# A Mamba scan phase with decays and half of h in PSUM, B times u on GpSimd, and a sum over states by accumulating transposes

## The reference

```python
def _mamba_block(x, ...):                    # 4 blocks: 0 then 1 forward, 2 then 3 backward
    xz = layer_norm(x) @ in_w                # 256 -> 2 x 512
    xs, z = split(xz)
    xc = silu(causal depthwise conv of 4 taps (xs) + conv_b)
    delta = softplus(xc @ xd_w @ dtp_w + dtp_b)          # 512 channels
    Bm, Cm = xc @ xB_w, xc @ xC_w                        # 16 states
    dA = exp(delta[..., None] * A)
    dBx = (delta * xc)[..., None] * Bm[:, :, None, :]
    h[t] = dA[t] * h[t-1] + dBx[t];  y[t] = sum over n of h[t, :, n] * C[t, n]
    return (y + D * xc) * silu(z) @ out_w + x
```

## Time and profile before

| | value |
|---|---|
| median of 3 runs | 11924.65 us (11923.49 to 11926.36) |
| the profiled execution | 11928.52 us, its span 11926.8 us |
| first scan to last scan of the Mamba phase | 116.9 to 10202.7 us |
| busy share over the span | DVE 89%, PE 84%, PEld 66%, ACT 51%, POOL 1% |
| mean granted TensorE clock | 0.919 of full speed |

### The profile page before, as it was taken

The page is one execution under the profiler, slowest core; times in us unless marked ns, Lnnn a source line. Parts: engine busy times, 40 slices in busy tenths (PEclk is TensorE's granted clock), DMA queues, the critical chain, the costliest instruction groups (busy, mean ns, idle before and its releaser), DMA issues. The chain is left out here.

```text
span 11926.8 us, 119277 instructions
## 1 busy us (share of the span) xinstructions
PE 10008.6 (84%) x40728; PEld 7855.0 (66%) x40728; DVE 10590.5 (89%) x8817; ACT 6109.2 (51%) x9969; POOL 94.9 (1%) x167
## 2 busy tenths in 40 slices
PE   7888888888888888888888888888888887799998
PEld 5666666666666666666666666666666666577776
DVE  6999999999999999999999999999999999333332
ACT  4555555555555555555555555555555554244443
POOL 0000000000000000000000000000000000000000
PEclk8999999999999898999999989999999998899999
DMA  2211122222211122212221222222221221000000
GB/s 79 76 63 59 68 77 71 70 72 70 76 64 63 64 76 71 77 67 75 71 69 50 76 71 75 69 70 75 71 69 57 67 71 65 22 11 11 11 11 9
DMA packets 357680, 728.02 MB, mean 61 GB/s; under 512 B 143670, under 2 KB 188890, under 8 KB 357082
## 3 DMA queue, kind: packets, MB, share of 16 engines
q1 hardware_dynamic: 343128, 683.98, 17.1%
q0 software_dynamic: 10240, 33.56, 0.8%
q10 hardware_dynamic: 3714, 2.89, 0.1%
HBM read 699.27 MB, written 21.05 MB: 60 GB/s over the span
## 5 line engine op out<-in xcount | busy, mean ns | idle before, releaser
L896 PE MATMUL y_ps<-hb,ident 128*128 128x257 f32 x16384 | 4489.7, 422 | 1478.3 <-DVE hb L692 1471.4
L896 PEld LDWEIGHTS y_ps<-hb,ident 128*128 128x128 f32 x16384 | 3286.5, 207 | 2497.1 <-DVE hb L692 1987.9
L683 DVE TENSOR_TENSOR_SCAN hb<-decay,hb 128x1028 f32<-128x1028 f32 x2048 | 4697.0, 2293 | 22.9 <-issue 22.2
L506 ACT ACTIVATE decay<-delta,neg_a 128x512 f32<-128x512 f32 x4096 | 2681.8, 712 | 2531.5 <-DVE hb L683 1804.7
L692 DVE TENSOR_TENSOR hb<-hb,c_all 128x1028 f32<-128x1028 f32 x2048 | 2505.2, 1223 | 0.0
L673 DVE TENSOR_TENSOR hb<-b_all,u_buf 128x1028 f32<-128x1028 f32 x2048 | 2471.7, 1207 | 5.8
L787 PE MATMUL w_ps<-xn,in_w 128*128 128x257 f32 x4096 | 1040.3, 402 | 146.5 <-ACT xn L407 116.7
L787 PEld LDWEIGHTS w_ps<-xn,in_w 128*128 128x128 f32 x4096 | 819.4, 202 | 306.0 <-issue 131.3
L787 PE MATMUL w_ps<-xs_pad,diag_store 128*128 128x257 f32 x4096 | 954.8, 379 | 0.2
L787 PEld LDWEIGHTS w_ps<-xs_pad,diag_store 128*128 128x128 f32 x4096 | 774.1, 189 | 114.2 <-ACT diag_store L427 1.0
L787 PE MATMUL w_ps<-sz,out_w 128*128 128x257 f32 x2048 | 517.7, 397 | 0.8 <-DVE sz L700 0.8
(11 more groups left out here) (237 smaller groups left out, 9233.5 us busy)
## 6 DMA issues: line engine op xcount, KB each, us to landing
b_all<-bc_dram SPq DMA_DIRECT2D x512, 514.0 KB, 3.6
c_all<-bc_dram SPq DMA_DIRECT2D x512, 514.0 KB, 4.9
in_w<-in_L_attn_in_w SPq DMA_DIRECT2D x64, 1024.0 KB, 4.9
x_in<-in_x POOLq DMA_DIRECT2D x128, 256.0 KB, 2.8
out_w<-in_L_attn_out_w SPq DMA_DIRECT2D x64, 512.0 KB, 3.7
h_mid<-h_cur SPq DMA_DIRECT2D x32, 257.0 KB, 3.2
h_F<-h_mid SPq DMA_DIRECT2D x16, 514.0 KB, 3.7
out<-o_sb SPq DMA_DIRECT2D x64, 86.0 KB
```

The costliest lines, as they stand in the source:

```text
L506: last = func(decay[:, u % NDA, i, :, 1:S], delta[:, c, :, 1:S], ACT.Exp, scale=neg_a[:, k, c, NU * n + i:NU * n + i + 1])
L683: dve.tensor_tensor_scan(h, decay[:, u % NDA, :, :, :].rearrange("p n b s -> p (n b s)"), h, 0.0, ALU.mult, ALU.add).then_inc(scan_done, 1)
L896: last = pe.matmul(y_ps[c % 2][:, b, 0:S], ident[:, :], hb[:, u % NHB, i, b, :], start=False, stop=(n == PAIRS - 1 and i == NU - 1))
```

## The change

- `decay` and the h of even states (`h_ps`) move to PSUM, as single states without token 0: `decay` has two buffers (NDP = 2), `h_ps` one. ACT writes one state's decays per instruction, two states ahead, between two halves of each unit's other work (`after_even`, `after_odd`).
- The scan runs per state and image: 256 columns, with token 0's B u as the initial value (an SBUF column). Even states' h goes to `h_ps`, odd ones' to `ch` in SBUF (NPR = 8 buffers). `c_times_h` is one instruction of 512 columns per state, from `h_ps` or in place, into `ch`.
- B times u goes to POOL, one instruction of 514 columns per state (`bu`, NBU = 4 buffers). So do the third part of `step_size`, `delta_x`, the convolution's diagonal matrices, `skip_weights`, and token 0's output (`first_tokens`, with `first_gains` on DVE).
- PE adds a state by four accumulating transposes (`is_transpose`) of 128 x 128 blocks of `ch` into one PSUM bank `y_ps`; tokens are on its partitions. At the end of a chunk ACT copies it to `y_t` (`token_rows`), PE turns it back into a `w_ps` buffer (`channel_rows`, keys y0 to y3), and DVE's `output` reads that.
- The loads of x move from POOL's queue to SP's.

The core of the diff:

```diff
+STATES = CI * NST
+L = S - 1
+NBU, NPR, NDP = 4, 8, 2
+POOL_C = ()
+        for name, before in [("y2", "dt0"), ("y1", "cv1" if jj in (2, 4) else "xs2")] + [("y0", "cen0" if jj == 4 else "var")]:
+    def y_at(jj):
+        return (12 if jj == 4 else 9), 18, (26 if jj in (2, 4) else 25)
+        y_ps = ctx.enter_context(nc.psum_tensor("y_ps", [P, 4, P], F32))
+        h_ps = ctx.enter_context(nc.psum_tensor("h_ps", [P, NB * L], F32))
+        decay = ctx.enter_context(nc.psum_tensor("decay", [P, NDP, NB * L], F32))
...
 # SP, period
                     load_weights(jj + 1)
+                    if jj == 2 and not is_final(g):
+                        load_x(g, 4)
                     bring_bc(g, jj + 1)
...
 # POOL
+            def b_times_u(g, jj, s):
+                if positive(job_count(g, jj, STATES, s + 1 - NBU)):
+                    pool.wait_ge(scan_done, job_count(g, jj, STATES, s + 1 - NBU))
+                pool.tensor_tensor(bu[:, s % NBU, :, :]..., b_all[:, n // NU, n % NU, :, :]...,
+                                   u_buf[:, c % 2, :, :]..., ALU.mult).then_inc(b_done, 1)
+                for s in range(STATES):
+                    b_times_u(g, jj, s)
+                    if s in (7, 9):
+                        step_size(g, jj, (s - 3) // 2)
+                    if s % NST == 11 and s < 3 * NST:
+                        delta_x(g, jj, s // NST + 1)
+                    if s in (21, 25):
+                        conv_weights(g, jj + 1, (s - 21) // 4)
+                    if s == 61:
+                        step_size(g, jj + 1, 0)
+                        delta_x(g, jj + 1, 0)
...
 # ACT
+            def token_rows(g, jj, c):
+                act.wait_ge(y_added, job_count(g, jj, STATES, NST * (c + 1)))
+                func(y_t[:, :, :], y_ps[:, :, :], ACT.Identity).then_inc(y_t_ready, 1)
+            def decays(g, jj, s):
+                if positive(job_count(g, jj, STATES, s + 1 - NDP)):
+                    act.wait_ge(scan_done, job_count(g, jj, STATES, s + 1 - NDP))
+                func(decay[:, s % NDP, :]..., delta[:, c, :, 1:S], ACT.Exp,
+                     scale=neg_a[:, k, c, n:n + 1]).then_inc(decays_ready, 1)
             def period(g, jj, first, last):
                 for u in range(UNITS):
+                        decays(g, jj, NU * u + NDP)
+                    after_even(g, jj, u, first, last)
+                        decays(g, jj, NU * u + NDP + 1)
+                    after_odd(g, jj, u, first, last)
...
 # DVE
+            def scan(g, jj, s, b):
+                inside = s % NU == 0
+                h = h_ps[:, :] if inside else ch[:, s % NPR, :]
+                last = dve.tensor_tensor_scan(h[:, cols], decay[:, s % NDP, cols], bu[:, s % NBU, b, 1:],
+                                              bu[:, s % NBU, b, 0:1], ALU.mult, ALU.add)
+            def c_times_h(g, jj, s):
+                product = ch[:, s % NPR, :]
+                h = h_ps[:, :] if s % NU == 0 else product
+                dve.tensor_tensor(product..., h..., c_all[:, n // NU, n % NU, :, 1:], ALU.mult).then_inc(c_done, 1)
             def period(g, jj, first, last):
+                    scan(g, jj, s, 0)
+                    scan(g, jj, s, 1)
                     if size:
                         step_size(*size, 0)
+                    scan(g, jj, s + 1, 0)
+                        scan(g, jj, s + 1, 1)
+                        c_times_h(g, jj, s)
+                        c_times_h(g, jj, s + 1)
+                    if u in y_at(jj):
+                        output(g, jj, y_at(jj).index(u))
...
 # PE
+            def add_state(g, jj, s):
+                if n == 0:
+                        pe.wait_ge(y_t_ready, job_count(g, jj, CI, c))
+                    for b, half, k in blocks:
+                        pe.matmul(y_ps[:, k, :], xc[:, jj % 2, c, b, 1 + half * P:1 + (half + 1) * P], skip_diag[:, :],
+                                  start=(k == 0), stop=False, skip_group_check=True)
+                for b, half, k in blocks:
+                    last = pe.matmul(y_ps[:, k, :], ch[:, s % NPR, k * P:(k + 1) * P], ident[:, :], is_transpose=True,
+                                     start=False, stop=(n == NST - 1 and k == 3), skip_group_check=True)
+            def channel_rows(g, jj, c):
+                pe.wait_ge(y_t_ready, job_count(g, jj, CI, c + 1))
+                    pe.wait_ge(read_of(name, g, jj), nth(name, g, jj) - 1)
             def period(g, jj, first, last):
+                        add_state(g, jj, NU * u - 2)
+                        add_state(g, jj, NU * u - 1)
+                    if u in y_at(jj):
+                        channel_rows(g, jj, y_at(jj).index(u))
```

More of the change, by code:

```diff
@@ L49, in one_job @@
     def one_job(jj, more):
-        keys = [("tmean", 4)] if jj == 3 and more else []
+        keys = [("y3", jj - 1)]
+        keys += [("tmean", 4)] if jj == 3 and more else []
         keys += [("o0", jj - 1), ("o1", jj - 1)]
@@ L549, in prepare_back, with first_input_at, after_even @@
                 projections(g, jj)
+            def first_input_at(jj):
+                return {2: 15, 4: 16}.get(jj, 13)
+            def after_even(g, jj, u, first, last):
+                if u == 0:
+                    softplus_start(g, jj, 3)
+                if u == 1:
+                    softplus_log(g, jj, 2)
+                if u % PAIRS == 0 and not (first and u == 0):
+                    token_rows(g, jj - (u == 0), (u // PAIRS - 1) % CI)
+                if u in (4 + (jj == 3), 5 + (jj == 3)) and not first:
+                    stream_out(g, jj - 1, u - 4 - (jj == 3))
+                if jj == 3 and not last and u == 6:
+                    inverse_deviation("tok", g, 4)
+                if u in (gates_at(jj) + 2, gates_at(jj) + 4):
+                    c = u - gates_at(jj) - 2
+                    gate(g, jj, c)
+                    gate(g, jj, c + 1)
+                    act.preload_act_table_set(LOG_EXP)
+                if last:
+                    return
+                if u == norm_at(jj) + 1:
+                    centred(g, jj + 1, 0)
+                if u == norm_at(jj) + 2:
+                    inverse_deviation("job", g, jj + 1)
+                if u in (first_input_at(jj), conv_at(jj) + 5):
+                    conv_input(g, jj + 1, 0 if u == first_input_at(jj) else 2)
+                if u in (conv_at(jj) + 3, conv_at(jj) + 8):
+                    c = (u - conv_at(jj) - 3) // 5 * 2
+                    conv_output(g, jj + 1, c)
+                    conv_output(g, jj + 1, c + 1)
+                    act.preload_act_table_set(LOG_EXP)
+                if u == conv_at(jj) + 10:
+                    projections(g, jj + 1)
+                if u in (26, 27):
+                    softplus_start(g, jj + 1, u - 26)
+                if u == 28:
+                    softplus_log(g, jj + 1, 0)
+                if u == 31:
+                    softplus_start(g, jj + 1, 2)
@@ new lines, in after_odd @@
+            def after_odd(g, jj, u, first, last):
+                if u == 0:
+                    softplus_powers(g, jj, 3)
+                if u == 1:
+                    softplus_log(g, jj, 3)
+                if jj == 3 and not last and u == 4:
+                    square_tokens(g, 4)
+                if jj == 0 and u == 6 or jj == 4 and u == 8:
+                    start_backward(g, jj + 1)
+                if jj == 4 and u == 11:
+                    copy_h(g, 4)
+                if last:
+                    return
+                if u == norm_at(jj) + 1:
+                    centred(g, jj + 1, 1)
+                if u == (15 if jj == 4 else 12):
+                    gain_and_bias(g, jj + 1)
+                if jj == 2 and not is_final(g) and u in (13, 15):
+                    tokens(g, 4, (u - 13) // 2)
+                if u in (first_input_at(jj), conv_at(jj) + 5):
+                    conv_input(g, jj + 1, 1 if u == first_input_at(jj) else 3)
+                if u in (26, 27):
+                    softplus_powers(g, jj + 1, u - 26)
+                if u == 28:
+                    softplus_log(g, jj + 1, 1)
+                if u == 31:
+                    softplus_powers(g, jj + 1, 2)
@@ L907, in lead_in @@
+                last.then_inc(full_of("first", 0, 0), 1)
                 pe.wait_ge(setup_act, 7)
```

420 lines of the change are left out of this document (226 added, 194 removed).

## The result

The changed kernel takes 12334.5 us (12324.3 to 12338.4) against 11924.1: a ratio of 1.0343 with a 95% interval of 1.0325 to 1.0361. It is 3.4% slower, as forecast in direction; the size was forecast at half, 12130. The profiled execution took 12324.3, its span 12322.5.

What follows compares the result with a forecast made beforehand. VectorE was taken to bound the Mamba phase at 157.7 us per job; 133.4 + 12.5 + 5.0 + 6.0 + 4.0 = 160.9 gave 12130 us, own range 11700 to 12500, over all 10950 to 12750.

Steps and rivals of the forecast that it cites:

- DVE's own work: VectorE's instructions in a Mamba job without waits on other engines: 133.4 us per job against 157.7, a gain of 24.3.
- POOL's hold of the odd C h: The odd state's C h, both inputs in SBUF, delayed by POOL's product: 0.39 us per unit, 12.5 per job.
- waits for decays, with PE's clock: DVE waiting on ACT's longer blocks with two decay buffers, 5.0 us per job, plus 4.0 for PE's slower clock.
- waits for POOL's B u: POOL's queue in the Mamba phase: no bound, 6 us ahead with four buffers, costed at nothing.
- waits before outputs: Chunk 0's output(0) waits for channel_rows: 7.8 us in three of four jobs, 0.4 in the fourth, mean 6.0.
- a share of the overlap: The odd C h loses 0.47 of its 0.63 us overlap with POOL's product: 0.29 us per unit.
- The second reading: DVE's odd C h is held until 0.14 us before POOL's product ends: 0.48 us per unit.
- rival 2: Odd C h held the whole 0.63 us by POOL, 7.7 us per job more: 12620 us, chance 0.18.
- clock term: PE, idle more, runs conv units at half clock: 8 us per job, taken at half, 4.0 (ends 0 and 8).
- Utilisation: Expected in the profile: PE busy near 60% with a mean clock under 0.85, POOL near 60%.
- 1: Rival: smaller waits, POOL's overlap at its share or nil, PE at full clock; 11670 to 10590 us, chance 0.33.
- 3: Rival: a PSUM operand doesn't free DVE, so scans meet POOL's products; 13380, at worst 15220 us; chance 0.05.

Runs made afterwards that it cites:

- taking one away alone: Changed kernel with either output(0) of VectorE two units later (12300.1 us), or y1 taken after cv1 for blocks 2 and 4 (12269.0 us).
- taking the hold away: Changed kernel with GpSimd's B times u cut to 16 columns of 514: 11561.5 us, ratio 0.9694 to the kernel before.
- the ring: Changed kernel with decays, h and product in three PSUM banks, scan in place, C h behind the next state's first scan: 11610.0 us, ratio 0.9738.
- three moves after the ring: The three-bank kernel plus output(0) two units later, y1 behind cv1, outputs' waits on themselves one scan later; the fastest version: 11249.1 us, ratio 0.9433.
- the C h in the new order: Changed kernel with every C h issued behind a scan (C h of s-1, then of s, between scans): 12269.4 us, ratio 1.0293.

## Why the prediction was right in sign and short in size

The forecast's job of 160.9 us came to 163.9. Per job:

| term | forecast | measured | from |
|---|---|---|---|
| DVE's own work | 133.4 | 132.4 | what is left of 163.9 |
| POOL's hold of the odd C h | 12.5 | 16.5 | (1197 - 680) ns x 32 |
| POOL's hold of L821 | 0 | 1.1 | (1212 - 681) ns x 128 / 64 |
| waits for decays, with PE's clock | 9.0 | 8.1 | 516.2 / 64 |
| waits for POOL's B u | 0 | 0.5 | 33.9 / 64 |
| waits before outputs | 6.0 | 5.3 | 338.1 / 64 |
| sum | 160.9 | 163.9 | |

(680 ns is what an odd C h takes beside constants only. The outputs' waits on themselves, 67.2 / 64 = 1.05, are in the first line, in the forecast as in the measurement.)

- *The step that was mis-sized is the hold.* The earlier trace rows allowed two readings, a share of the overlap (0.29 per unit) and a hold until 0.14 us before POOL's end (given as 0.48, rightly 0.49); I took the middle, 0.39, which no mechanism gives. In the unit shown the product ends at 5022.73, 0.87 after the odd C h starts, and this takes 1.42 where 0.68 would do: 0.74, which is 0.13 before POOL's end. At the share of 0.47 it would be 0.41. The second reading is right, here and in the 1762 cases counted above. The remaining length is more than the forecast's 0.63 because this product takes 1.29 and not the 1.09 of the earlier trace rows. In two of four chunks it is the short one, and a clean hold is 0.54.

  The mean hold, 0.52, is lower than both since POOL's other work shifts its products: 271 odd C h take under 0.70, others meet only the end of a product. So the second reading's 0.49 would have given a time near 12335, and that would have been partly luck, longer holds and missed ones making up for each other.

  The Trainium skill (SBUF — State Buffer, Summary: rules for kernel authors) says that the second of the two fully blocks until the first has finished: the runs agree but for the last 0.13 us, in both directions (POOL's 1.63 beside a C h that began first). They also agree with the statement of the Trainium skill (SBUF — State Buffer, Who interferes with whom) that an instruction of GpSimd that only writes doesn't contend. That was rival 2; its mechanism is the one that holds, its time of 12620 was too high for the mean hold.
- *POOL's hold of `step_size`*, 1.1 per job, was in no term: L821 on `cen` and `sq` has two SBUF inputs as well, and I had counted only the C h.
- *DVE's own work* was right: scans of 723 and 738 ns, 0.65 apart (forecast 0.66), and 0.58 between the two products (0.60). A unit without the hold takes 3.77 (forecast 3.84). That is in line with a pointer initial value at the 0.05 of the earlier trace rows, though no run left it out, and a PSUM result costs 0.015 us at most.
- *The output of chunk 0* was right in place and near in size: 335 of the 338 us stand there, in one wait per job, 5.6 to 7.2 on average in three of four jobs (forecast 7.8) and 1.0 in the fourth (0.4).
- *The decays* were right in the sum, 8.1 for 9.0, by luck in good part. By the unit at which DVE waits, the first `conv_output` costs 3.2 per job (forecast 1.3), the second 1.1 (2.0), `conv_input` 1.7 (0.5), the gates 0.5 (1.2). Another 1.4 stand at u = 6 and 7 in the last job of a group, behind `stream_out` and the tokens' normalization, which I had not looked at. The half of a clock term that made the sum fit has no row of its own: no run shows what the clock costs. And the chain of `y1` and cv1 was not in it; I had asked of each product which read it waits for, but not for the products whose buffer a new key shifts.
- *Utilisation*: PE 74% where I had said near 60%, a miss; its mean clock 0.82 (under 0.85); POOL 51% for near 60%.
- *Rivals*: 1 needed a small hold and no clock loss, and neither came. 3 fell: scans beside POOL's products keep 723 ns, and only with decays in SBUF do they go to 1152.
- *Why the removed work brought nothing*: DVE's own work fell by 157.7 - 132.4 = 25.3 us per job, and holds and waits took 31.5. The waits are partly interchangeable: taking one away alone gave 34 or 65 us, taking the hold away 773 or, by the ring, 724, and three moves after the ring another 361.

What stays open: how much PE's clock costs by itself (no run held it up); what the third bank is worth without the rest of the ring; why a POOL product of this form has two prices; and, in the fastest version, the 554 us for which DVE still waits for decays.

## What to carry to other kernels

Before work moves to GpSimd, list VectorE's instructions with two SBUF inputs and lay them beside GpSimd's in a timeline: each one that starts under a GpSimd product waits nearly to that product's end. So put one operand of each into PSUM, or count the remaining length of the product and not a share of it.

When a wait is removed and the time hardly moves, read the idle time before every other group of the same engine: the wait may have hidden another engine's work. When instructions of one engine change places, look at when each buffer now comes free and when it is needed again: here 2.4 us became 1.8, once the hold is left out of the sum. And when an experiment leaves something out, count it in the trace: the table loads had only moved, and just that made the run instructive.

A new name in a rotation of shared buffers changes the buffer of every name after it, so write out who waits for whom again for all of them.

## What the runs showed of the hardware

- The hold is mutual and goes by who is first: VectorE's product of two SBUF inputs 0.68 to 1.42 us behind GpSimd, GpSimd's 1.27 to 1.63 behind VectorE. Its size is what is left of the product that came first, less 0.13 us where VectorE is held (1762 cases in the changed kernel), and less 0.14 where GpSimd is (the middle of 1570 cases with the C h in the new order).
- A scan with its decays in PSUM, B u in SBUF and its initial value in an SBUF column isn't held: the 5273 that meet POOL work take 727 ns on average.
- GpSimd's product of 514 columns has two prices, some 1.10 and 1.27 to 1.31 us, also where nothing holds it. Inside a chunk they alternate from state to state, and from one chunk to the next they change places: where the number of the state and that of the chunk (from 0) are both even or both odd, the product is never under 1.25 us (2048 of 2048, in the changed kernel and in the ring version); of the others most are under 1.15 (1984 and 1918 of 2048). In the ring version:

```profile
5003.65 1.27 POOL L448 TENSOR_TENSOR bu<-b_all,u_buf 128x514 f32<-128x514 f32 x1 [0.24 <-DVE decay L833]
...
5005.75 1.09 POOL L448 TENSOR_TENSOR bu<-b_all,u_buf 128x514 f32<-128x514 f32 x1 [0.83 <-DVE decay L833]
...
5007.64 1.27 POOL L448 TENSOR_TENSOR bu<-b_all,u_buf 128x514 f32<-128x514 f32 x1 [0.79 <-DVE decay L833]
```

  The state's number decides where B and `bu` lie in SBUF, the chunk's where u lies. That their places beside each other are the cause is a guess that no run tested.
- A constant written by GpSimd over 514 columns takes 0.53 us, half a product, and holds no C h (1550 cases).
